# A two-block transformer kernel: per-piece order lists behind layer 0's self-attention, 32-row window matmuls, and S^T of the first heads issued by four

## The reference, cut to what matters

```
# layer 0
x = x + gate_a * (softmax(q k^T / sqrt(8)) v @ W_proj + b)        # q,k,v from modulate(ln(x)); 512 x 512 per head
x = x + softmax(q_c k_c^T / sqrt(8)) v_c @ W_cproj + b            # q_c from ln(x), k_c,v_c from ln(context), 77 keys
x = x + gate_m * (gelu(modulate(ln(x)) @ W_mlp1 + b) @ W_mlp2 + b)
# layer 1 (m = silu(mod) @ w_ada + b_ada gives nine shifts, scales and gates)
x = x + g_msa * window_attention(ln(x)*(1+sc)+sh)                 # tokens rolled by 32, windows of 64, 16 heads
x = x + g_mca * topk_cross_attention(ln(x)*(1+sc)+sh, context)    # softmax over the 16 largest of 77 scores
x = x + g_mlp * ((silu(a) * b) @ w_m2 + b_m2)                     # a, b = halves of ln(x)*(1+sc)+sh @ w_m1 + b_m1
```

## Time and profile before

| | us |
|---|---|
| median of 3 runs (lowest, highest) | 476.36 (472.24, 478.07) |
| the profiled execution, its own time | 460.53 |
| its span, from the first to the last instruction | 458.7 |
| PE, DVE, ACT, POOL busy in the span | 374.1, 297.2, 204.3, 111.9 |

### The profile page before, as it was taken

One profiled execution on the slowest core, in us unless ns is written; L12 is line 12 of the kernel. 1 busy time (PEld: TensorE's weight loads), 2 busy tenths in 40 slices (PEclk: granted clock), 3 DMA queues, 4 the chain that ended last, 5 costly groups with the idle time before them and its releaser, 6 DMA issues.

```text
span 458.7 us, 8982 instructions
## 1 busy us (share of the span) xinstructions
PE 374.1 (82%) x3317; PEld 210.5 (46%) x3317; DVE 297.2 (65%) x1279; ACT 204.3 (45%) x303; POOL 111.9 (24%) x130
## 2 busy tenths in 40 slices
PE   3999899999989987899888889978574566675985
PEld 2325412223333155677655567754353344454454
DVE  4648556999897056666338361235989999997342
ACT  1311126666756935666432123332453555653511
POOL 5332304910010011001015100011434544444010
PEclk9965659999999999999999585566877877776999
DMA  7544625110000000000000000000000000000000
GB/s 201 37 157 120 186 59 156 53 55 2 3 1 2 0 1 1 1 2 1 1 1 2 4 1 7 3 3 1 1 1 1 2 2 1 1 1 1 1 24 24
DMA packets 13247, 12.88 MB, mean 28 GB/s; under 512 B 2373, under 2 KB 11681, under 8 KB 13203
## 3 DMA queue, kind: packets, MB, share of 16 engines
q1 hardware_dynamic: 13007, 12.28, 10.3%
q0 software_dynamic: 160, 0.01, 0.0%
q10 hardware_dynamic: 36, 0.01, 0.0%
HBM read 9.41 MB, written 2.63 MB: 26 GB/s over the span
## 4 chain that ended last, share of the span: by engine, by line
PE 57%; DVE 29%; ACT 7%; issue 5%; POOL 1%; DMA 1%; SPq 0%; ACTq 0%; DVEq 0%; POOLq 0%
PE psum L1491 6%; PE psum L1561 5%; PE psum L1529 5%; DVE left L1284 4%; DVE left L1291 4%; PE psum L1514 4%; DVE mx L1210 4%; PE psum L1355 3%; PE psum L1660 3%; DVE top L1281 3%; DVE top L1288 3%; PE psum L1508 3%; PE psum L1485 2%; PE psum L1544 2%; PE psum L1628 2%
## 5 line engine op out<-in xcount | busy, mean ns | idle before, releaser
L1210 DVE TENSOR_REDUCE mx<-psum 128x1 f32<-128x512 f32 x128 | 81.4, 684 | 26.4 <-PE psum L1491 18.0
L803 ACT ACTIVATE big<-psum 128x1024 f32<-128x1024 f32 x64 | 62.5, 1022 | 46.1 <-PE psum L1514 25.2
L607 POOL TENSOR_TENSOR rstd<-vareps,minus_half 128x4 f32<-128x4 f32 x12 | 12.2, 1020 | 178.8 <-DVE vareps L969 178.7
L1561 PE MATMUL psum<-kblk,qf 128*128 128x308 f32 x128 | 46.0, 490 | 1.1 <-DVE qf L1157 0.8
L1572 PE MATMUL psum<-ident,pr 128*77 128x128 f32 x256 | 38.3, 299 | 10.5 <-POOL pr L725 10.5
L1491 PE MATMUL psum<-KS,QS 72*128 72x512 bf16 x112 | 43.0, 417 | 3.0 <-DVE mx L1210 2.3
L1572 PEld LDWEIGHTS psum<-ident,pr 128*77 128x77 f32 x256 | 34.4, 167 | 18.4 <-POOL pr L725 13.9
L725 POOL TENSOR_TENSOR pr<-pr,early 128x616 f32<-128x616 f32 x16 | 23.9, 1493 | 55.8 <-ACT early L909 37.8
L1529 PE MATMUL psum<-big,V 128*9 128x512 f32 x256 | 34.3, 609 | 0.5 <-ACT big L803 0.5
L1584 PE MATMUL psum<-QS,vc 77*9 77x128 f32 x256 | 13.9, 342 | 24.1 <-ACT QS L919 24.0
L1514 PE MATMUL psum<-QS,KS 75*128 75x512 bf16 x112 | 32.8, 379 | 0.4
(11 more groups left out here) (202 smaller groups left out, 687.3 us busy)
## 6 DMA issues: line engine op xcount, KB each, us to landing
QS<-scr_q SPq DMA_DIRECT2D x7, 288.0 KB
KS<-scr_k SPq DMA_DIRECT2D x7, 288.0 KB
scr_q<-qp SPq DMA_DIRECT2D x2, 384.0 KB, 2.9
scr_k<-kp SPq DMA_DIRECT2D x2, 384.0 KB, 3.6
gates<-scr_g SPq DMA_DIRECT2D x2, 320.0 KB, 4.1
early<-in_L_xcond_w_ada_dram SPq DMA_DIRECT2D x1, 576.0 KB, 5.1
scr_k<-kp SPq DMA_DIRECT2D x2, 256.0 KB, 4.3
wmlp<-in_L_xcond_W_mlp_dram SPq DMA_DIRECT2D x2, 256.0 KB, 3.2
```

Source lines behind the costliest of these rows:

```text
L803: freed(act.activation(pT[:, u % 2, 1024 * half:1024 * (half + 1)], ps, ACT.Exp), "sT", 0, u, half)
L1210: freed(dve.tensor_reduce(mx[:, n % 3, at:at + 1], ps, AX_X, ALU.max), "max", t, q)
L1561: last = pe.matmul(ps[:, 512 * a:512 * a + HH // 2 * S], qf[:, b, i * P:(i + 1) * P], kb[:, c0:c0 + HH // 2 * S], start=True, stop=True)
```

## The change

Layer 0's self-attention keeps its loop, with two edits. EARLY moves m01, gate0, mods and gate1 from t = 4, 5, 6 and 6 to t = 9, 10, 11 and 13 and into other rooms (the ring Y), and SP's `spread_gates` moves behind the maximum rows of the third group with them. `first_halves` issues both halves of a unit of the first group together at q = 1, four matmuls on four groups of 32 rows.

Behind it, loops become three lists of pieces, `pe_order`, `dve_order` and `act_order`, and the rooms are dealt from the first. What moves by them:

- layer 0's cross-attention: DVE's res10, stat20 and norm20 one half earlier (13, 13, 14);
- batch 1's window projections go chunk by chunk between batch 0's maxima; batch 1's maxima go between the units of batch 0;
- S4, the first unit that needs batch 1's maxima, stands ahead of out30; "S6 V5 W4" ahead of qc10, "S7 V6 W5" ahead of the first top-16 scores (W is the units' turn, T before);
- batch 0's oT30, out40, lnT50 and its gated MLP stand in halves 10 to 15, its gate products in DVE's list behind halves 14 and 15; the MLP's second products take a room of two banks for two chunks; out50 stands between the last turn D and oT31;
- D comes one half earlier in layer 1; layer 1's scores use room W0 alone.

Window maxima and window S read 32 rows where they read 8 and 9. `wqkF` moves from `left` to `V`, the window copies get a buffer of their own (`oraww`), and POOL's context blocks for layer 1 are built a batch at a time, earlier.

```diff
-EARLY = {0: ("ln",), 1: ("qk",), 2: ("v0",), 3: ("v1",), 4: ("ctx", "m01"), 5: ("kv", "gate0"), 6: ("mods", "gate1")}
+EARLY = {0: ("ln",), 1: ("qk",), 2: ("v0",), 3: ("v1",), 4: ("ctx",), 5: ("kv",), 9: ("m01",), 10: ("gate0",),
+         11: ("mods",), 13: ("gate1",)}
...
+def pe_order():
...
+    order += [("wqk", 0, c) for c in range(NQ)] + pieces("wv0 max000 max001 lnT31")
+    order += [("wqk", 1, 0)] + pieces("max010 max011") + [("wqk", 1, 1)] + pieces("max020 max021")
+    order += [("wqk", 1, 2)] + pieces("max030 max031") + [("wqk", 1, 3)] + pieces("mT0 wv1 max100 max101 max110")
+    order += pieces("S0 S1 V0 max111 S2 V1 W0 max120 S3 V2 W1 max121 max130 V3 W2 max131 W3 mT1 "
+                    "oT20 S4 out30 S5 V4 lnT40 S6 V5 W4 qc10 S7 V6 W5")
+    ahead = {0: "V7 W6", 1: "W7", 10: "oT30", 13: "lnT50"}
+    behind = {2: "oT21", 3: "out31", 4: "lnT41", 5: "qc11", 10: "out40"}
+    for e in range(-1, HALVES + 1):
+        found, turns = cross_pieces(e, 1)
+        order += found + pieces(ahead.get(e, "")) + turns + pieces(behind.get(e, ""))
+        order += [("mlp1", 0, e - 13)] if e in (13, 14) else []
+    order += [("D", 1, B * NT - 1)] + pieces("out50 oT31 out41 lnT51") + [("mlp1", 1, 0), ("mlp1", 1, 1)] + pieces("out51")
...
+    inside = {2: "W7", 11: "res40 stat50", 12: "norm50"}
+    behind = {1: "W6", 3: "res31 stat41", 4: "norm41", 5: "qc11", 14: "gate00 gate01", 15: "gate02 gate03"}
...
+    behind = {5: "lnT41", 10: "oT30", 14: "mlp100 mlp101", 15: "mlp102 mlp103"}
...
+def first_halves(j, q):
+
+    if not 0 <= j < UNITS:
+        return ()
+    if j < NT:
+        return (0, 1) if q == 1 else ()
+    return (q,) if q < 2 else ()
...
-                                                     QF[q0:q0 + D, b, c, t0:t0 + WIN], KF[q0:q0 + D, b, c, t0:t0 + WIN],
...
+                                             QF[q0:q0 + QUAD, b, c, t0:t0 + WIN], KF[q0:q0 + QUAD, b, c, t0:t0 + WIN],
...
-                                                     KF[q0:q0 + DV, b, c, t0:t0 + WIN], QF[q0:q0 + DV, b, c, t0:t0 + WIN],
...
+                                                 KF[q0:q0 + QUAD, b, c, t0:t0 + WIN], QF[q0:q0 + QUAD, b, c, t0:t0 + WIN],
```

More of the change, by code:

```diff
@@ L92, with pieces, cross_pieces @@
 GATE_SPAN = ((0, 2), (2, 5))
+def pieces(text):
+    return [tuple([word.rstrip("0123456789")] + [int(d) for d in word[len(word.rstrip("0123456789")):]])
+            for word in text.split()]
+def cross_pieces(e, layer):
+    last = B * NT * 2
+    found = [("sc", layer, e + 1)] if e + 1 < last else []
+    turns = [("T", layer, e - 1)] if 1 <= e <= last else []
+    if e % 2 == 0 and 1 <= e // 2 <= B * NT:
+        turns.append(("C", layer, e // 2 - 1))
+    if layer == 0 and e % 2 == 0 and e >= 4:
+        turns.append(("D", layer, e // 2 - 2))
+    if layer == 1 and e % 2 and e >= 3:
+        turns.append(("D", layer, (e - 3) // 2))
+    return found, turns
@@ L693, in _ @@
                     pool.tensor_tensor(crstd[:, :], cve[:, :], minus_half[0:S, 0:B], ALU.pow).then_inc(s_crs, 1)
-            ctx_blocks(0)
-            spread_qk()
+            pool.wait_ge(s_const, 4)
+            wait_read(pool, "kc")
+            for b in range(B):
+                ctx_blocks(0, b)
             gate_outputs()
@@ new lines, in _ @@
+            for b in range(B):
+                if b == 0:
+                    ln_out(0, 0)
+                    wait_read(act, "vecs")
+                    rows_k_out()
+                k_out(b)
+                q_first(b)
+                if b == 0:
+                    ln_out(0, 1)
+                k_mid(b)
+                q_mid(b)
+            ps = read_room(act, "ctxT")
+            freed(act.activation(ctxT[:, :, :], ps[:, 0:2 * B * S].rearrange("p (l n) -> p l n", l=2), ACT.Copy), "ctxT")
@@ new lines, in turned_weights_out @@
+            def turned_weights_out(layer, f):
+                s = f // 2
+                if s >= 2 and f % 2 == 0:
+                    wait_full(act, "pvc", layer, s - 2)
+                for part in range(2):
+                    ps = read_room(act, "pT", layer, f, part)
+                    h0 = HH * (f % 2) + 4 * part
+                    freed(act.activation(pcT[:, s % 2, h0:h0 + 4, :], ps[0:S, :].rearrange("p (h t) -> p h t", t=P),
+                                         ACT.Copy), "pT", layer, f, part)
@@ new lines, in hidden @@
+            def hidden(layer, b, c):
+                ps = read_room(act, "mlp", layer, b, c)
+                if layer == 0:
+                    v = VECS["L0_b_mlp1"] + c
+                    ins_ = act.activation(gT[:, b, c, :], ps, ACT.Gelu_apprx_tanh, bias=cols[:, v:v + 1])
+                else:
+                    v = VECS["L1_b_m1"] + c
+                    if c == 2:
+                        wait_read(act, "mlpb", b, 0)
+                    ins_ = act.activation(sa[b][c % 2], ps, ACT.Silu, bias=cols[:, v:v + 1])
+                freed(ins_, "mlp", layer, b, c)
```

1055 lines of the change are left out of this document (505 added, 550 removed), and 6 rows, old and new, of the table EARLY_ROOMS.

## The result

The changed kernel's ratio to the kernel before is 1.0207, 95% interval [1.0153, 1.0261]. Over all 20 executions of each the medians are 471.27 (464.50 to 476.59) and 472.84 (457.52 to 482.21). Thirteen of those of the kernel before, at 470 to 482, ran in a slower state and the ratio leaves them out, which is why it and the medians differ. The other seven (457.52 to 464.84) have a mean of 461.4, the changed kernel's ten shortest (464.50 to 470.26) one of 468.5, a ratio of 1.015. So it is slower by 1.5 to 2%; that it is more than 2% is not shown. The forecast was 464.2, 12.2 us less than 476.36.

What follows compares the result with a forecast made beforehand. The prediction saw no single bound: TensorE or DVE, depending on the stage. Its terms -4.7 + 1.2 - 6.5 (windows) + 2.0 - 4.2 = -12.2, put on the median 476.36, gave 464.2, range 449 to 476.

Steps and rivals of the forecast that it cites:

- The base: The median of 476.36 from which the forecast subtracted 12.2 us; the profiled execution was 460.53.
- Early edits, -4.7: Layer 0's self-attention: columns moved later (-3.0, +3.2) and S^T by four (-4.9), together 4.7 us saved.
- Cross-attention, +1.2: Layer 0's cross-attention: res10 to the statistics one half earlier on DVE delays the last turn, costing 1.2 us (0 to 2.3).
- To S0, -11.8: Windows, first step: batch 1's projections fill gaps between batch 0's maxima, so S0 starts 11.8 us earlier.
- The rival of the fallen clock: Batch 1's projections run at 1.2 GHz from 252 on, window term near 0, total 470.7; chance 0.19.
- oT20 to the first MAX8, +5.5: Windows, third step: units standing ahead of qc10 and the scores add 5.5 us; out30 behind S4 no change.
- The halves, +2.0: Top-16 halves: DVE work added inside, less some present stalls, costs 2.0 us (0.5 to 4).
- The end, -4.2: Last half to oT31 takes 11.8 us instead of 16.0, saving 4.2 (-5.5 to -2); nothing won after oT31.
- 32 rows, 0: Window S and maxima reading 32 rows: 0 taken, with the clock raised by the rows kept as a rival.
- The slower side: Rival: TensorE at a granted clock near 0.5 bounds the top-16 halves, total 479.7, slower than before; chance 0.06.

Runs made afterwards that it cites:

- e13: The kernel before with layer 0's two early self-attention edits alone, repeated with more rounds: 457.01, ratio 0.9927 to the kernel before.
- e2: The kernel before with layer 0's two early self-attention edits alone, first run: 461.63, no ratio of its own.
- e14: The changed kernel with res10, stat20 and norm20 put back by one half in layer 0's cross-attention: 469.68, ratio to before 1.018.
- e7: The changed kernel with S4 to S7 dealt both rooms W0 and W1 in place of W1 alone: 466.39, ratio to before 1.011.
- e8: The changed kernel with the edits of e14, e7 and e3, and out30 ahead of S4: 455.33, ratio to before 0.986.
- e9: e8 with batch 0's gated MLP and gate products back behind the halves, and out50 behind out41: 452.70.
- e12: e9 with two out-projections' residuals and statistics moved behind the half, and what hangs on them by a half: 453.69, ratio to before 0.988.
- e1: The changed kernel again, no edit, for a second trace and more times: 472.97.
- e3: The changed kernel with DVE's division D read half a step later, and batch 0's end one half later: 463.85.
- e11: The changed kernel with 8 and 9 rows in place of 32 in window maxima and S: 472.63.
- e6: The kernel before with window maxima and window S reading 32 rows, nothing else: 467.13.
- e10: The kernel before with layer 0's two early edits and the 32 rows, nothing else of the change: 451.94.
- e4: The changed kernel with batch 0's chain (out30, qc10, first scores) moved ahead among units 4 to 7: 471.51.

## Why the forecast was wrong, step by step

*The base: the number lay in its range by luck.* 464.2 was put on 476.36, the median of three executions at 472 to 478, where seven of the later ones are at 457.5 to 464.8. So 471.27 is 5 below that base, and inside 449 to 476, though the kernel is slower than the one before.

*Early edits, -4.7: right, a little large.* -3.4 in the whole (e13); the S^T of the first group is 5.2 to 5.6 shorter (e2, e13), where 4.9 was taken. The choice that four S^T take a pair's time is what the rows show. Up to the out-projection thirteen traces with these edits have 199.4 to 207.9, three without them 206.9 to 209.1.

*Cross-attention, +1.2: mis-sized, 3.4 to 4.4 by e14.* I moved 2.3 us of DVE work and allowed half of it. What stood behind the wait was right; what it set off was not counted: "The last turn moves by up to 2.3" left out that DVE waits 2.22 for the out-projection itself, a time that it spent on the next half's scores before, and that TensorE, idle behind it, comes back at the low clock (1.91 for 1.04).

*To S0, -11.8: right, -9.4.* The rival of the fallen clock did not come: 1.00 through both rows of that stretch.

*oT20 to the first MAX8, +5.5: failed, +8.0 here.* The step "out30 is queued behind S4 on TensorE, as behind three steps before: no change" missed that S4 to S7 are dealt one room. That line of the dealing was in the diff. It also left out that out30 inherits S4's wait for the rows (3.44): out30 starts 7.1 after oT20, where I had about 4.4. Of the 8, two rooms give 5.6 back (e7); with out30 ahead of S4 as well the stretch is 18.5, 19.0 and 18.2 (e8, e9, e12), against 19.0 before. In these three S6 V5 W4 still stand ahead of qc10, and S7 V6 W5 ahead of the scores, from which the whole of the +5.5 was made; they cost nothing that shows, at a granted clock of 0.64 to 0.72 (0.59 and 0.50 in the two traces of before). So the size came near by luck: the cost stood in the step that I had put at nothing.

*The halves, +2.0: failed, +10.3. This is the largest error.* The step was "Added inside: one more division D (0.55)". DVE's added work came out near. From the first MAX8 to the end of the last MATCH_REPLACE8, before and then changed (e1):

```profile
316.06:418.61 102.55, 64.83 (x533) 44.72 (x531) 99.23 (x808) 50.59 (x85) 44.72 (x34) 0.80 0.00 1
```

```profile
317.93:430.87 112.94, 74.66 (x520) 51.54 (x521) 101.84 (x815) 58.81 (x94) 45.85 (x35) 0.74 0.00 1
```

Busy, 2.6 were added where I had 3.2; idle went from 3.3 to 11.1, where I took 1.2 off. I counted D's own time, not its wait. On TensorE D comes one half earlier (e = 3, not 4), but DVE reads it behind half 3 where it was half 5, two earlier, and the chain from a half's last MATCH_REPLACE8 through ACT, POOL, TensorE, ACT, TensorE does not fit: 9.4 of waits (e1), of which 1.0 is left with e3; of the halves' 6.4 that e3 wins, some 5 are waits and 1.5 the gate products that left. I named neither what DVE waits for nor what is queued behind it, and took DVE's list to be as elastic as it was.

*The end, -4.2: failed, +0.6 over both rows.* I had 11.8 to oT31; it is 14.0. The last exponentials' left part ran at 433.87, 3.0 behind the halves' end, where before it was 0.04 behind, because Silu with its table and the return to the exponential's stand ahead of it. Before, then the changed kernel (e1):

```profile
418.65 0.81 ACT L909 ACTIVATE early<-left,negbig 128x616 f32<-128x616 f32 x1 [2.36 <-DVE left L1291]
```

```profile
428.00 1.28 ACT L1009 ACT_TABLE_LOAD   x1
...
431.95 1.28 ACT L978 ACT_TABLE_LOAD   x1
...
433.87 0.79 ACT L985 ACTIVATE early<-left,negbig 128x616 f32<-128x616 f32 x1
```

I allowed 1.3. My upper bound of 14 to oT31 was met, but not by out50 at the low clock: it took 3.74 there as before. That out50 "hid there, so nothing is won" was right, but its going cost: with it behind oT31 the clock had been at 0.93 to 1.00, without it 0.82 to 0.86. The loads at 428.00 and 431.95 are 1.28 each and stand on the chain that ends last, and the activation behind each starts 0.01 later: no drain, as the forecast took it. The Trainium skill's "ScalarE: Activation LUTs" (Table sets: the hidden batching unit) advises to batch activation calls by table set. This trace agrees, at 1.28 for each load.

*32 rows, 0: right for this kernel within 3 us (e11), wrong for the kernel before (e6, e10).* The row I weighed, the 32-row S^T at 0.50, did not decide it.

*The rivals.* The slower side was named through TensorE at 0.5 in the halves. The clock there was 0.74 and DVE stayed the bound; the loss came by its waits. So the sign was on the table with 6 in 100, with the wrong mechanism.

## What to carry to other kernels

When an in-order engine's reading of a result is moved earlier, write down the chain that makes the result, its length, and what is queued behind the reading; its own 0.55 us is the least of it. Read the dealing of buffers as part of the order: one room where two took turns turned 1.65 into 3.0. When one engine's list is changed, move the others' with it: e4 lost 3.7 to a division left where it was. And filling an engine's gaps at one place may take away work that hid a wait, or went with a full clock, at another.

## What the runs showed of the hardware that was not expected

Reading 32 rows instead of 9, with the same columns and count of matmuls, went with a granted clock of 0.88 and 1.00 from 286 to 294, where four traces with 9 rows have 0.50. Over both orders the clock was back at 1.00 before oT20 in nine of eleven traces with 32 rows, and in none of five with 8 and 9. Why it is so, and why two of the eleven lack it, was not isolated.
